# One rank-1 scatter between groups in place of two, and null rows laid down ahead of each expert's list

## The reference, cut to what matters

```python
x = x + _L0_gnn_ref(xn, src, dst, ...) + _L0_mix_ref(xn[None], ...)[0]
x = x + _L0_ffn_ref(_layernorm(x)[None], ...)[0]
...
probs = softmax(logits); rw, re = top_k(probs, 2)        # 8 experts
out = tokens
for e in range(8):
    out = out + combine[:, e:e + 1] * (gelu(tokens @ w1[e] + b1[e]) @ w2[e] + b2[e])
```

## Time and profile before

| | us |
|---|---|
| median of 3 runs | 515.15 |
| lowest, highest | 514.3, 517.36 |
| the profiled execution, its own time | 517.46 |
| the profiled execution, its span | 515.7 |
| mean granted TensorE clock | 0.899 |
| TensorE busy, share of the span | 86% |
| GpSimd busy, share of the span | 46% |

### The profile page before, as it was taken

One profiled execution on the slowest core, in us unless ns is written; L12 is line 12 of the kernel. 1 busy time (PEld: TensorE's weight loads), 2 busy tenths in 40 slices (PEclk: granted clock), 3 DMA queues, 4 the chain that ended last, 5 costly groups with the idle time before them and its releaser, 6 DMA issues.

```text
span 515.7 us, 10120 instructions
## 1 busy us (share of the span) xinstructions
PE 441.4 (86%) x3269; PEld 345.3 (67%) x3270; DVE 325.9 (63%) x878; ACT 271.6 (53%) x620; POOL 235.1 (46%) x258
## 2 busy tenths in 40 slices
PE   2999999978999999999996398740499999999992
PEld 1788887854666655666654287730498999999981
DVE  3676648754777767777741767762087888766661
ACT  1775554545777766777661458600244444444440
POOL 5035864443111111111210008788567764688884
PEclk9999999975999999999999665555599999999997
DMA  8705210936576655566673002335555543466752
GB/s 217 168 5 164 83 27 2 324 81 146 122 132 130 129 128 128 129 129 128 128 128 65 1 1 76 91 105 144 140 154 170 176 138 114 86 110 114 125 89 25
DMA packets 122450, 58.72 MB, mean 114 GB/s; under 512 B 95797, under 2 KB 119585, under 8 KB 122398
## 3 DMA queue, kind: packets, MB, share of 16 engines
q1 hardware_dynamic: 107262, 42.29, 35.1%
q0 software_dynamic: 13744, 14.39, 12.9%
q10 hardware_dynamic: 1392, 1.39, 1.1%
HBM read 19.14 MB, written 20.34 MB: 77 GB/s over the span
## 4 chain that ended last, share of the span: by engine, by line
PE 73%; DMA 8%; DVE 7%; ACT 5%; POOL 3%; issue 2%; SPq 1%; POOLq 0%; DVEq 0%; ACTq 0%
PE bank L1432 12%; PE bank L1245 11%; PE bank L1443 11%; PE bank L1234 9%; PE bank L1170 4%; DMA region_a<-region_a 4%; PE bank L1276 4%; PE bank L1180 3%; PE bank L1183 3%; PE bank L1421 3%; PE bank L1377 3%; POOL xs L544 2%; DMA rows<-in_x 2%; PE bank L1256 2%; PE bank L1192 2%
## 5 line engine op out<-in xcount | busy, mean ns | idle before, releaser
L628 ACT CAST region_a<-bank 128x500 bf16<-128x500 f32 (+1 forms) x175 | 112.0, 667 | 50.2 <-PE bank L1234 44.6
L544 POOL DMA_INDIRECT xs<-rows,slot_i x50 | 61.6, 1232 | 53.7 <-issue 49.7
L1245 PE MATMUL bank<-region_a,region_z 125*64 125x500 bf16 (+1 forms) x525 | 71.7, 369 | 3.1 <-DMA region_a<-region_a 3.1
L1234 PEld LDWEIGHTS bank<-region_a 128*128 128x128 bf16 x625 | 42.6, 104 | 47.4 <-issue 32.9
L1234 PE MATMUL bank<-region_a 128*128 128x125 bf16 x625 | 67.0, 227 | 4.7 <-ACT region_a L628 2.2
L518 POOL COPY wide<-den 125x256 f32<-125x256 f32 x25 | 11.4, 456 | 129.9 <-DVE den L930 129.9
L1432 PE MATMUL bank<-region_a,region_c 128*128 128x128 f32 x512 | 69.9, 280 | 0.7 <-ACT region_a L693 0.6
L1443 PE MATMUL bank<-region_c,region_a 128*128 128x256 f32 x256 | 66.2, 381 | 0.0
L1432 PEld LDWEIGHTS bank<-region_a,region_c 128*128 128x128 f32 x512 | 63.9, 196 | 1.5 <-ACT region_a L693 0.8
L562 POOL DMA_INDIRECT out<-region_a x32 | 55.9, 1747 | 11.5 <-issue 9.1
L1105 DVE COPY region_c<-region_w 128x1026 f32 x64 | 45.9, 717 | 22.0 <-issue 21.1
(11 more groups left out here) (215 smaller groups left out, 795.2 us busy)
## 6 DMA issues: line engine op xcount, KB each, us to landing
region_a<-xs SPq DMA_DIRECT2D x64, 130.5 KB
region_w<-in_w SPq DMA_DIRECT2D x4, 1024.0 KB, 9.7
rows<-in_x SPq DMA_DIRECT2D x5, 560.0 KB
xs<-null SPq DMA_DIRECT2D x2, 913.5 KB, 7.7
xs<-null SPq DMA_DIRECT2D x12, 130.5 KB, 4.8
ztab<-region_z SPq DMA_DIRECT2D x5, 234.4 KB
out<-region_a POOLq DMA_INDIRECT x64
xs<-rows,slot_i POOLq DMA_INDIRECT x50, 4.0
```

Source lines behind the costliest of these rows:

```text
L544: nc.gpsimd.indirect_dma_start(xs, bass.IndirectOffsetOnAxis(slot_i[:, t, r2:r2 + 1], 0), rows[:, t, :], None).then_inc(sent[r2], 16)
L628: nc.scalar.copy(to, chunk_ps[n % 2][:, 0:w * TP].rearrange("p (c t u) -> p c t u", c=w, t=NT)).then_inc(adj_done, 1)
L1234: last = nc.tensor.matmul(chunk_ps[n % 2][:, (c - lo) * TP:(c - lo + 1) * TP], loh[:, t % 2, c, :], koh[:, t % 2, c, 0:TP], start=True, st ...
L1245: last = nc.tensor.matmul(block_out(b), zparts[:, t, part, :], adjT[0:TP, t % 2, lo:hi, 0:TP], start=False, stop=False, skip_group_check=True)
```

## The change

Three things are changed together.

1. The order of the sends: one rank-1 tile follows the five rank-0 tiles of a group (BETWEEN = 1), and the tiles sent before the experts start end with tile 12 (EARLY = 13). Twelve rank-1 tiles in place of ten are left for the time between the chunks' scatters.
2. The chunks of a list are counted from its end. The last chunk ends with the list, and the first one begins up to 127 rows before it. Each list now starts 128 rows into its area (`base` is P), and those 128 rows are null rows, stored by two more DMAs on SyncE's queue in the first stage. `store_pad`, its 16 stores, `rows_known` and the waits on `pads_stored` are gone.
3. The table of chunks is worked out with other operations: `list_row` is the row at which chunk 0 would have to stand for each expert, `to_next` its differences, and the first row is a sum over the experts already passed.

```diff
-BETWEEN, EARLY = 2, 15
+BETWEEN, EARLY = 1, 13
...
-        def store_pad(eng, r2, e):
-            at = eng.value_load(pad_of[0:1, r2 * NX + e:r2 * NX + e + 1], min_val=0, max_val=2 * RR - P)
-            eng.dma_start(xs[bass.ds(at, P), :], null[:]).then_inc(pads_stored[r2], 16)
...
+                lists = xs[r2 * RR:r2 * RR + NX * CAP, :].rearrange("(e n) d -> n e d", e=NX)
+                sp.dma_start(lists[0:P], null[:].rearrange("p (a d) -> p a d", a=1).to_broadcast([P, NX, ROW])
+                             ).then_inc(nulls_stored, 16)
...
-            sp.wait_ge(rows_known, 1)
-            for e in range(NX // 2):
-                store_pad(sp, 0, e)
             sp.wait_ge(table_done, 1)
-            sp.wait_ge(nulls_stored, 32)
-            sp.wait_ge(pads_stored[0], NX * 16)
+            sp.wait_ge(nulls_stored, 64)
             sp.wait_ge(sent[0], NT * 16)
             for c in range(NCH):
                 if c == MC:
-                    sp.wait_ge(pads_stored[1], NX * 16)
                     sp.wait_ge(sent[1], NT * 16)
                 load_chunk(c)
-                if XB <= c < XB + 2 * NX and c % 2 == 0:
-                    store_pad(sp, 1, (c - XB) // 2)
...
-                nc.gpsimd.iota(base[:], [[RR, 2], [CAP, NX]], base=0, channel_multiplier=0,
+                nc.gpsimd.iota(base[:], [[RR, 2], [CAP, NX]], base=P, channel_multiplier=0,
...
+                nc.gpsimd.iota(list_row[:, :, NX], [[RR, 2]], base=NX * CAP + NULLS * P - MC * P, channel_multiplier=0,
...
-            act.wait_ge(rows_known, 1)
-            for e in range(NX // 2, NX):
-                store_pad(act, 0, e)
...
+            chain(nc.vector.scalar_tensor_tensor(list_row[:, :, 0:NX], ends[:], -float(P), list_row[:, :, 0:NX],
+                                                 ALU.mult, ALU.add))
+            chain(nc.vector.tensor_tensor(to_next[:], list_row[:, :, 1:NX + 1], list_row[:, :, 0:NX], ALU.subtract))
             for r2 in range(2):
                 last = nc.vector.tensor_tensor(past[:, r2, :, :], past[:, r2, :, :],
-                                               ends[:, r2:r2 + 1, :].to_broadcast([1, MC, NX]), ALU.mult)
+                                               to_next[:, r2:r2 + 1, :].to_broadcast([1, MC, NX]), ALU.mult)
             chain(last)
-            chain(nc.vector.tensor_reduce(prior[:], past[:], AX_X, ALU.max))
-            chain(nc.vector.scalar_tensor_tensor(first_row[:], prior[:], -float(P), chunk_row[:], ALU.mult, ALU.add))
-            chain(nc.vector.scalar_tensor_tensor(first_row[:], expert_f[:], float(CAP), first_row[:], ALU.mult, ALU.add))
+            chain(nc.vector.tensor_reduce(prior[:], past[:], AX_X, ALU.add))
+            for r2 in range(2):
+                last = nc.vector.scalar_tensor_tensor(first_row[:, r2, :], prior[:, r2, :], list_row[:, r2, 0:1],
+                                                      chunk_row[:], ALU.add, ALU.add)
+            chain(last)
```

More of the change, by code:

```diff
@@ L39 @@
 MC = 32
-BETWEEN, EARLY = 2, 15
+BETWEEN, EARLY = 1, 13
 XB = 6
 NCH = 2 * MC
-CAP = N + P + 3
+CAP = P + N + 3
 NULLS = MC - -(-N // P)
@@ L199, in build @@
         chunk_of = sb("chunk_of", [1, MC])
-        chunk_row = sb("chunk_row", [1, 2, MC])
+        chunk_row = sb("chunk_row", [1, MC])
+        list_row = sb("list_row", [1, 2, NX + 1])
+        to_next = sb("to_next", [1, 2, NX])
         stats = sb("stats", [TP, NT, 6])
@@ L254, in build @@
         row_of = sb("row_of", [1, 2 * MC], I32)
-        pad_of = sb("pad_of", [1, 2 * NX], I32)
         edges_in, z_in, gnn_in, q_in, kv_in, mix_in, ffn_in = map(sem, (
@@ L289, in build @@
             "t3_ready", "tkT_done", "lg_ready", "lg_read", "diff_done", "ex_done", "oh_done", "pos_ready", "pos_read"))
-        slot_done, cum_done, cnt_ready, rows_known, table_done = map(sem, (
-            "slot_done", "cum_done", "cnt_ready", "rows_known", "table_done"))
+        slot_done, cum_done, cnt_ready, table_done = map(sem, (
+            "slot_done", "cum_done", "cnt_ready", "table_done"))
         sent = [sem(f"sent{r2}") for r2 in range(2)]
-        pads_stored = [sem(f"pads_stored{r2}") for r2 in range(2)]
         xch_in = [sem(f"xch_in{s}") for s in range(XB)]
@@ L459, in set_tables @@
                                allow_small_or_imprecise_dtypes=True)
-                nc.gpsimd.iota(chunk_row[:], [[RR, 2], [P, MC]], base=0, channel_multiplier=0,
+                nc.gpsimd.iota(list_row[:, :, NX], [[RR, 2]], base=NX * CAP + NULLS * P - MC * P, channel_multiplier=0,
+                               allow_small_or_imprecise_dtypes=True)
+                nc.gpsimd.iota(chunk_row[:], [[P, MC]], base=0, channel_multiplier=0,
                                allow_small_or_imprecise_dtypes=True).then_inc(rows_set, 1)
@@ L1071, in _ @@
             chain(nc.vector.tensor_copy(held_of[:], counts))
-            nc.vector.tensor_tensor(pad_of[:].rearrange("p (r x) -> p r x", r=2), held_of[:],
-                                    base[0:1, :].rearrange("p (r x) -> p r x", r=2), ALU.add).then_inc(rows_known, 1)
+            nc.vector.tensor_tensor(list_row[:, :, 0:NX], held_of[:], base[0:1, :].rearrange("p (r x) -> p r x", r=2),
+                                    ALU.add)
             chain(nc.vector.tensor_scalar(nch[:], held_of[:], 1.0 / P, (P - 1.0) / P - 0.5 + 0.25 / P, ALU.mult, ALU.add))
```

## The result

The changed kernel takes 513.09 us (median of 20 runs, 507.04 to 518.66), the kernel before 515.01 (20 runs, 513.12 to 517.36). The ratio is 0.9947, interval 0.9929 to 0.9965: faster by 0.4 to 0.7%, which is within 1%. The ratios of this document are taken over the fast runs alone, without those that lie over 1.5% above the fastest of their kernel (six of these 20), and the medians over all runs, so the medians lie 1.9 us apart here where the ratio stands for 2.7. The forecast was 510.4, the range 508.0 to 513.5.

The account below looks back on a forecast made before the run. The prediction took GpSimd's queued sends to bound the seam and TensorE to set the pace behind it. It summed -5.2 at the seam and +0.5 in the first stage to -4.7, from 515.15 to 510.4 us, range 508.0 to 513.5.

Parts of the forecast that it names:

- Part 1: Seam between routing and experts: four fewer GpSimd sends ahead of the last rank-0 tile, first chunk 5.2 us earlier.
- Part 5: First stage: new null-row stores delay the gathers that VectorE, then TensorE, wait for; 0.5 us lost, bounds 0 and 2.3.
- first rival: Short group 2 wait, earlier clock rise or missing pads' 0.6 us, no first-stage loss: -6.5, 508.7 us; chance 0.24.
- Part 2: Experts' first pass: twelve sends between scatters in place of ten, no lag, 10 us of loaded chunks before chunk 32; cost 0.
- Part 3: Pad stores ahead of the first load and between loads vanish: taken as 0, with 0 to 0.6 us kept as gain.
- Part 4: Chunk table done 0.3 us later, covered by the sends by 8 us: cost 0.
- The null stores cost in the first stage: Rival: gathers land with the stores, the third 4 us late, TensorE loses 2.3: -2.9, 512.3 us; chance 0.16.
- TensorE's clock: Experts' start: 2.4 GHz comes 10.2 us after the first load; two us earlier or later is -1 or +1; no shift taken.
- slower: Rival: GpSimd falls behind in the first pass, a pair taking 5.2 us, 8.1 us lost: 518.6 us; chance 0.04.
- the change doesn't do what it says: Rival: at the seam another of SyncE's waits ends last, table or nulls late by 8 us: 515 us; chance 0.04.
- More than forecast: Rival: larger gain from short group 2 wait, earlier clock or missing pads, no first-stage loss: 508.7 us; chance 0.24.

Follow-up runs that it names:

- second set: Runs on the 515 chip, with the kernel before at 515.10 us, the change at 512.09, and list stores ahead of SyncE's wait for the codes at 509.37.
- the stores early: Changed kernel with both null-row list stores moved ahead of SyncE's wait for the codes: 509.37 us, ratio 0.9895 to the kernel before.
- second execution: Another profiled execution of the unaltered changed kernel, 510.63 us; that run's median was 512.09 us, ratio 0.9955 to the kernel before.
- (0, 11): BETWEEN, EARLY = 0, 11 in place of 1, 13, in the changed kernel with list stores ahead of SyncE's codes wait: 514.97 us, ratio 0.9995.
- the stores alone: Kernel before plus two first-stage stores of 8 x 128 null rows into a buffer nothing reads: 531.77 us, ratio 1.0136.
- (2, 15): BETWEEN, EARLY of the kernel before; put into the changed kernel: 530.81 us, ratio 1.0102, or 524.06 us, 0.9953, with the list stores early.

## Why the prediction was right and wrong

The time lies in the range, 2.7 us above the forecast (513.09 against 510.4). The mechanisms of Part 1 and Part 5 are the ones that the traces show; the step that failed is the size of Part 5's term.

That the number lies in the range is in part luck. By the second set's traces of the change and of the kernel before, the two terms of the sum come to 3.3 us gained at the seam and 2.0 lost by the first send, 1.3 in place of 4.7. The rest of the 4.9 us between the spans are gains that the sum put at nothing: 0.8 until the first scatter and 1.1 in the first pass, which the first rival had in part, and 1.8 at the end of the program, which no part of the prediction had (0.15 is lost again in the second pass). Without them, an estimate from these traces, the time would be some 3.5 us higher and above the range. By its own steps, the sizes from the 515 chip:

- **Part 1, -5.2.** Right in mechanism, a little too large. The wait ahead of the 13th send is there (gap 1.37 in place of the 0.30 + 1.1 = 1.4 of the text), the 25th has none, and the copies hit two sends ahead of the 29th. The first send to the last rank-0 one is 48.41 - 43.81 = 4.6 us shorter with the stores early. Against the forecast base, 49.38, it is 5.6: the base was an execution with three sends of 1.54 to 1.69 us, where the second one of the same kernel has two, of 1.43 and 1.44. The load follows 0.24 later than before, so 4.4 is left, inside the bounds of 4.3 and 6.8. In the second execution of the change it is 3.3, below the bounds, by a wait that Part 1 hadn't looked for: group 1's positions come 10.13 us after group 0's there, in place of 8.24 in the trace that it was worked out from (316.34 - 308.10), and the 7th send has a gap of 1.27 (above). The two sends hit by copies took 0.33 and 0.27 us more than 1.19 (1.52 and 1.46), though each overlaps some 0.9 us of copies; so the trace again shows less than the Trainium skill (SBUF — State Buffer, SBUF: two separate sides), by which a send would be held as long as a copy runs.
- **Part 2, 0.** Right for this change: a pair of scatters and a send takes 416.05 - 411.83 = 4.22 us, the idle time of 1.05 us comes back with chunk 24, nothing waits at chunk 32. But its reason was wrong. The run with (0, 11) shows 7.1 us of loaded chunks ahead of chunk 32 in place of 10, and the load after the last landing takes 430.39 - 427.7 = 2.7 of them: a last tile that lands 4.4 us after SyncE asks for it is already late.
- **Part 3, 0 (gain 0 to 0.6).** Too small. TensorE's busy time between 392 and 418 us is 26.00 in place of 25.39, and the first 32 chunks take 66.37 - 65.42 = 0.95 us less. That they come from the missing pad stores is argued, not shown: the wait of 0.61 us is in both traces with pads and in none of the three without, but the one run without pads and with the old sends (0.9953) is from the other chip, whose first pass is another matter.
- **Part 4, 0.** Right: the table never shows.
- **Part 5, +0.5 (bounds 0 and 2.3).** This is the step that failed. Measured: 2.7 us by the medians and 3.1 by the ratios, above the upper bound but not clear of it by this pair of kernels; on the 526 chip it is 6.8 (530.81 against 524.06) and clear. Two things went wrong. I let the third gather land 2.2 us later, at most 4, and it landed 5.3 later (10.2 after its issue in place of 4.9), 3.6 later in the second execution (8.5). And I priced the third alone, while VectorE waited for the first, which had 58.20 - 55.3 = 2.9 us of room: it landed 7.6 and 6.2 us later than its 5.3 after issue. In the second execution, where the clock doesn't fall, this closes: L778 starts 61.34 - 58.08 = 3.26 us later, less the 0.9 of gaps 2.4, and the reduction starts 67.42 - 64.93 = 2.5 later. Behind both lies the end of the stores, taken as 56 to 58 us at 351 GB/s. In the first execution they kept that rate only until 46 us; it was 273 to 295 GB/s up to 54 us and some 200 from there, and they ended at 64.2 in the first execution and 59.0 in the second. The gathers landed from 0.9 us before that end to 4.5 after it, near to what the rival *The null stores cost in the first stage* had, though it too had the stores done at 58. Its time, 512.3 us, is the nearest to the result. The Trainium skill's rule (DMA: Bandwidth & Descriptors, Queues, rings and completion order), that the engines take turns between queues packet by packet, spoke for the smaller loss, and I let it weigh. The gathers took 1.9 to 2.4 times as long as before (8.8 to 12.9 us in place of 4.6 to 5.3), 1.5 to 2.2 times in the second execution. That doesn't refute turns; what failed is my step from turns to a small loss. With one store moved away they took 5.1 to 5.3.
- **TensorE's clock, no shift.** At the seam the clock rose sooner after the load: 10.2 us in the first trace of before and 9.3 in the second, 8.2 with the stores early, 8.3 and 7.9 in the two traces of the change. The first scatter follows the load 0.66 us sooner, 11.55 to 10.89, a small gain that fits it. The first rival had this. The clock mattered elsewhere: in the profiled execution the wait of 3.74 us in the first stage was followed by a grant of 0.50 for some seven us, and its loss was 6.8 us at the reduction against 2.5 in the execution with a wait of 2.15. The price of the stores thus differs between executions. The changed kernel's times are wider spread in the first comparison (11.6 us against 4.2 of the kernel before), but not in the second set (5.4 against 5.7), so that this comes from the clock isn't shown.
- **The end**, not in the sum: 6.98 to 5.25, -1.7 us (below).

In the traces of the 515 chip, before against early stores: first send +0.5, seam -4.4, first scatter -0.66, first pass -0.95, second pass +0.20, end -1.73, together -7.0, which is the difference of the spans. By the medians it is 5.7; single executions differ by a us or two. The change as it stands gives back 2.7 to 3.1 of that by its times, and 2.1 by its span, of which 1.5 stand at the first send; the gap ahead of the 7th adds 1.0, and the later parts give 0.4 back.

The *slower* rival is refuted by the pair time, and *the change doesn't do what it says* by the seam. *More than forecast* would have been the result had the stores stood elsewhere: 509.37 against its 508.7.

## What to carry to other kernels

Work taken off the critical stretch by an unconditional store elsewhere isn't free because the queue that issues it is idle: look at what is in flight when it drains, and count on a small indirect DMA beside the stores to land about when they end or some us after (0.9 before to 4.5 after here), with the stores themselves slower than when they run alone. Price the first operation that waits, not only the last. A free slot is visible in the windows (the DMA engines stood still from 34 to 40 us even with the early stores), and moving two stores there was worth about as much on the 515 chip as the change brought without it (2.7 and 3.0 us by the medians). A wait that was harmless for one order of sends has a margin that must be measured in loaded buffers; when sends are moved behind it, work that margin out first.

## What the runs showed that I had not expected

- **A burst of stores loses rate, and beside gathers more of it.** 346 GB/s from 44 to 46 us, 273 to 295 until 54, with no gather issued before 50.35, and 195 to 207 with both in flight, at a DMA share of 1.00 or more throughout. In the trace of the stores alone the rate is down to 191 from 48 to 50 us, before its first gather. So the gathers aren't the whole cause, and the rest of it is open. The loss isn't proportional to the bytes: one store of 1 MB leaves none, two cost 2.7 us and more.
- **The end of the program depends on the order of the sends.** From the start of the last scatter to the end of the span it is 6.96 to 7.05 us in all five traces with (2, 15), with or without the rest of the change, and 4.93 to 5.25 in all nine others. The last scatter has landed after 2.7 us in both kinds (kernel before and early stores, second set). SyncE's last wait, in the kernel before and in the changed one:

```profile
SPq L55 <- PEq L55: 4.0, 1, 4.0
```

```profile
SPq L55 <- PEq L55: 2.2, 1, 2.2
```

  Why it does is open; no run was made for it. It is some 1.75 us of every gain told above of a version with other sends than (2, 15), and on the 526 chip more than half of the 3 us that the new sends bring.
- **Two chips, 11 us apart**, with the same kernel (515.10 and 525.52 to 526.29 us), by stalls of several engines at once in the first pass of the experts. The two chips also seem to disagree on what a part is worth: the change with its stores out of the gathers' way is worth 1% on one (0.9895, 0.9860 to 0.9930) and 0.6% on the other (0.9943, 0.9917 to 0.9968). The stores stand at two different places in these, early and late, and the early version wasn't run on the 526 chip. There the sends alone (0.9943, 0.9942) and the rest with the old sends (0.9953) come out like the whole, but with intervals of 0.3 to 0.4% to either side they can't be ranked.
